# A recurrence kernel on one core: mixing, feeding and projecting in 64x64 tiles of the array, row halves added by VectorE, both projections ahead of the turn

## What is computed

```python
ms = mean(tokens ** 2, -1); x = tokens * rsqrt(ms + 1e-4) * norm_w     # 16 heads of 16
a_t = tanh(a)                                                          # (16 heads, 64, 64)
def step(state, x_t):                                                  # state: (batch, 16, 64)
    state = tanh(einsum('bhs,hst->bht', state, a_t) + einsum('bhd,hds->bhs', x_t, b))
    mixed = einsum('bhs,hsd->bhd', state, c) + skip * x_t
    return state, mixed
out = tokens + outs @ w_out.T + b_out                                  # then x = layernorm(x + out)
```

## Time and profile before

| | |
|---|---|
| runs | 2425.71 us median, 2422.68 to 2427.81 |
| profiled execution | 2422.44 us, its span 2420.7 us |
| mean granted clock | 0.980 |
| TensorE busy | 2310.3 us (95%) |
| VectorE busy | 1646.1 us (68%) |
| ScalarE busy | 1073.9 us (44%) |
| GpSimd busy | 1156.5 us (48%) |
| recurrence, first to last tanh | 1650.5 to 2204.9 us |

### The profile page before, as it was taken

How to read it: one execution, slowest core, us unless ns; L and a number is a source line. 1 busy time by engine, 2 the same in 40 slices (tenths; PEclk the granted TensorE clock), 3 DMA queues, 4 the chain that set the end, 5 groups by cost and what they waited for, 6 DMA issues and landing times. The chain is left out here.

```text
span 2420.7 us, 87690 instructions
## 1 busy us (share of the span) xinstructions
PE 2310.3 (95%) x35328; PEld 1553.8 (64%) x35328; DVE 1646.1 (68%) x4605; ACT 1073.9 (44%) x2707; POOL 1156.5 (48%) x1610
## 2 busy tenths in 40 slices
PE   6999999999999999869999999998999999997997
PEld 3565555556556665436666666666777777775775
DVE  3688888888877777548888888872444444443897
ACT  2656556665566666522222222222444444442444
POOL 2444454444444444337777777762333443331333
PEclk8999999999999999989999999997999999998999
DMA  2111111111111111020000000000100001101232
GB/s 86 56 36 44 45 45 45 45 45 41 45 45 45 45 45 36 28 69 27 31 30 30 30 30 26 31 22 22 35 30 30 30 30 34 31 28 46 79 87 78
DMA packets 91382, 100.88 MB, mean 42 GB/s; under 512 B 8625, under 2 KB 78033, under 8 KB 91217
## 3 DMA queue, kind: packets, MB, share of 16 engines
q1 hardware_dynamic: 91216, 98.67, 12.4%
HBM read 48.31 MB, written 33.55 MB: 34 GB/s over the span
## 5 line engine op out<-in xcount | busy, mean ns | idle before, releaser
L1427 ACT ACTIVATE r_state<-ps_state 128x64 f32<-128x64 f32 x1024 | 228.7, 223 | 335.6 <-PE ps_state L1524 330.0
L1521 PE MATMUL ps_state<-r_state,later_pairs_a 64*64 64x32 f32 x8192 | 340.9, 221 | 18.5 <-ACT r_state L1427 12.7
L1521 PEld LDWEIGHTS ps_state<-r_state,later_pairs_a 64*64 64x64 f32 x8192 | 287.6, 135 | 99.8 <-issue 81.4
L1524 PE MATMUL ps_state<-r_state,later_pairs_a 64*64 64x32 f32 x8192 | 340.9, 222 | 0.0
L399 DVE CUSTOM_DVE_ANT_0 ps_near<-ps_near,mask 128x512 f32<-128x512 f32 (+1 forms) x512 | 270.5, 590 | 92.3 <-PE ps_near L495 92.3
L273 POOL TENSOR_SCALAR_AFFINE_SELECT probsT<-probsT 128x512 f32<-128x512 f32 x256 | 159.4, 635 | 315.3 <-ACT probsT L382 173.6
L1524 PEld LDWEIGHTS ps_state<-r_state,later_pairs_a 64*64 64x64 f32 x8192 | 284.8, 135 | 0.0
L399 DVE CUSTOM_DVE_ANT_0 ps_far<-ps_far,mask 128x384 f32<-128x384 f32 (+1 forms) x512 | 198.8, 461 | 47.4 <-PE ps_far L495 46.4
L1234 PE MATMUL ps_down<-kept_w_downT,f_hT 128*128 128x256 f32 (+1 forms) x768 | 190.5, 390 | 1.9 <-ACT f_hT L1146 1.9
L1141 ACT ACTIVATE f_silu<-ps_gate 128x704 f32<-128x704 f32 x64 | 48.5, 757 | 313.8 <-PE ps_gate L1226 310.3
L503 PE MATMUL ps_far<-Q,K 32*128 32x256 f32 (+2 forms) x1536 | 175.8, 414 | 0.7 <-ACT probsT L379 0.5
(11 more groups left out here) (209 smaller groups left out, 5368.1 us busy)
## 6 DMA issues: line engine op xcount, KB each, us to landing
k_swap<-k_sin SPq DMA_DIRECT2D x128, 128.0 KB, 2.0
xT<-in_xT_dram SPq DMA_DIRECT2D x16, 512.0 KB, 3.6
xtok<-in_x_dram SPq DMA_DIRECT2D x16, 512.0 KB, 3.8
x_rows<-x SPq DMA_DIRECT2D x16, 512.0 KB, 2.8
f_x<-x_rows SPq DMA_DIRECT2D x64, 128.0 KB, 2.0
x_rows<-f_x SPq DMA_DIRECT2D x64, 128.0 KB, 1.7
r_x<-x_rows SPq DMA_DIRECT2D x64, 128.0 KB, 2.0
x_rows<-r_x SPq DMA_DIRECT2D x64, 128.0 KB, 1.9
```

The source lines that it names most:

```text
L1427: nc.scalar.activation(state[:, j % 2, banks, :, t, 0, :], sums[:, j % 2, banks, :, now], ACT.Tanh).then_inc(state_ready[t], 1)
L1521: nc.tensor.matmul(sums[half(v), j % 2, stays, c, now], A[half(v), 3 * q, c, :], last[half(v), stays, c, :], start=False, stop=True, skip_ ...
L1524: out = nc.tensor.matmul(sums[half(1 - v), j % 2, changes, c, now], A[half(v), 3 * q + 1 + was, c, :], last[half(v), changes, c, :], start ...
```

## The change

`pairs_b` and `pairs_c` get zeros, so that each product takes 64 rows of the array instead of 32 (feed) or 128 (mix), and 64 columns instead of 32 (mix). `project` becomes four matmuls, one for each quadrant. Where the contraction spans 128 rows (mix, project), upper and lower rows give separate sums in separate banks, and VectorE adds these with one more operation each. The banks of MIX and OUT change for that. PROJECTS and TURNS change places, VectorE adds z ahead of xT, and TensorE waits for its own last feed (inputs_in) in front of a tile's first step.

```diff
@@ LaterWeights
-        self.pairs_b = sb("pairs_b", [P, 2 * CC, STATE])
-        self.pairs_c = sb("pairs_c", [P, 6, CC, 2 * HEAD_DIM])
+        self.pairs_b = sb("pairs_b", [P, 2, 2 * CC, STATE])
+        self.pairs_c = sb("pairs_c", [P, 6, CC, 4 * HEAD_DIM])
@@ recurrence
-    TURN, MIX, OUT = 0, (1, 3), 2
+    TURN, MIX, OUT = 0, ((1, 3), (0, 2)), (1, 3)
@@ VectorE
-                            nc.vector.scalar_tensor_tensor(outs[:, s, c, :], xT[:, s, c, :], skip[:, c:c + 1], room[:, s, MIX[c], 0:P],
-                                                           ALU.mult, ALU.add).then_inc(outs_ready, 1)
+                            nc.vector.scalar_tensor_tensor(outs[:, s, c, :], xT[:, s, c, :], skip[:, c:c + 1], room[:, s, MIX[c][0], 0:P],
+                                                           ALU.mult, ALU.add).then_inc(outs_half, 1)
+                            dve.wait_ge(outs_half, 2 * i + (c - 1))
+                            nc.vector.tensor_tensor(outs[:, s, c, :], outs[:, s, c, :], room[:, s, MIX[c][1], 0:P], ALU.add).then_inc(outs_ready, 1)
+                        dve.wait_ge(out_full, i + 1)
+                        dve.wait_ge(twice_ready, i)
...
+                        nc.vector.tensor_tensor(z[:, s, :], room[:, s, OUT[0], :], x_twice[:, s, :], ALU.add).then_inc(z_half, 1)
+                        dve.wait_ge(z_half, i)
+                        nc.vector.tensor_tensor(z[:, s, :], room[:, s, OUT[1], :], z[:, s, :], ALU.add).then_inc(z_added, 1)
                     if exists(i, 1):
...
                     if exists(i, -1):
-                        dve.wait_ge(out_full, i + 1)
-                        dve.wait_ge(twice_ready, i)
...
-                        nc.vector.tensor_tensor(z[:, s, :], room[:, s, OUT, :], x_twice[:, s, :], ALU.add).then_inc(z_added, 1)
@@ TensorE, feed
-                        for v in range(2):
-                            for bank in range(BANKS):
-                                rows = slice(32 * bank, 32 * bank + 32)
-                                xT_now = xT[rows, s, c, :]
...
+                        for odd in range(2):
+                            for v in range(2):
+                                for r in range(2):
+                                    bank, weights_of = 2 * r + odd, B[half(r), odd, 2 * c + v, :]
+                                    xT_now = xT[half(r), s, c, :]
...
@@ project
-                    out = nc.tensor.matmul(room[:, s, OUT, :], outs[:, s, c, :], w_outT[:, c, :], start=(c == 0), stop=(c == CC - 1))
+                    for cols in range(2):
+                        for r in range(2):
+                            out = nc.tensor.matmul(room[half(cols), s, OUT[r], :], outs[half(r), s, c, half(cols)], w_outT[half(r), c, :],
+                                                   start=(c == 0), stop=(c == CC - 1), skip_group_check=True)
@@ mix
+                    for n in range(3):
+                        for cols in range(2):
+                            for r in range(2):
+                                into = room[half(cols), s, MIX[c][r], 0:P]
+                                weights_of = C[half(r), 3 * cols + n, c, :]
+                                if n == 0:
+                                    nc.tensor.matmul(into, weights_of, state[half(r), s, 2 * cols, c, :, 0, :], start=True, stop=False, skip_group_check=True)
+                                else:
+                                    out = nc.tensor.matmul(steps_of(into, n - 1), weights_of, state[half(r), s, 2 * cols + 1, c, n - 1::2, 0, :],
+                                                           start=False, stop=True, skip_group_check=True)
...
-                MIXES, PROJECTS, TURNS, FEEDS = (1, 3), (5, 9), 7, (13, 15)
+                MIXES, PROJECTS, TURNS, FEEDS = (1, 3), (5, 7), 9, (13, 15)
...
+                                if t == 0 and q == 0:
+                                    await_count(inputs_in, this_tile)
                                 recur(j, t, q, states)
```

More of the change, by code:

```diff
@@ L1459, in step @@
                                 dve.wait_ge(out_full, i - 1)
-                            nc.vector.scalar_tensor_tensor(outs[:, s, c, :], xT[:, s, c, :], skip[:, c:c + 1], room[:, s, MIX[c], 0:P],
-                                                           ALU.mult, ALU.add).then_inc(outs_ready, 1)
+                            nc.vector.scalar_tensor_tensor(outs[:, s, c, :], xT[:, s, c, :], skip[:, c:c + 1], room[:, s, MIX[c][0], 0:P],
[4 more added lines that the diff above has]
+                        dve.wait_ge(twice_ready, i)
+                        if later(i, -1, 2):
+                            dve.wait_ge(x3_ready, i - 2)
+                        nc.vector.tensor_tensor(z[:, s, :], room[:, s, OUT[0], :], x_twice[:, s, :], ALU.add).then_inc(z_half, 1)
+                        dve.wait_ge(z_half, i)
+                        nc.vector.tensor_tensor(z[:, s, :], room[:, s, OUT[1], :], z[:, s, :], ALU.add).then_inc(z_added, 1)
                     if exists(i, 1):
@@ L1533, in feed @@
                     for parity in range(2):
-                        for v in range(2):
-                            for bank in range(BANKS):
-                                rows = slice(32 * bank, 32 * bank + 32)
-                                xT_now = xT[rows, s, c, :]
[L1538 to L1543, removed]
+                        for odd in range(2):
[3 more added lines that the diff above has]
+                                    xT_now = xT[half(r), s, c, :]
+                                    if odd:
+                                        out = nc.tensor.matmul(steps_of(sums[half(v ^ parity), s, bank, c, :], parity), weights_of, steps_of(xT_now, parity),
+                                                               start=(c == 0 and parity == 0), stop=False, skip_group_check=True)
+                                    elif parity == 0:
+                                        nc.tensor.matmul(sums[half(v), s, bank, c, :], weights_of, xT_now,
+                                                         start=(c == 0), stop=False, skip_group_check=True)
                     return out
@@ L1601, in step @@
                                 if before:
-                                    fill(j, OUT, 9, c == 0)
+                                    fill(j, OUT[0], 9, c == 0)
                                 if c == 0:
@@ L1624, in recurrence_arrays @@
     pairs_a = np.zeros((P, 6, CC, STATE), np.float32)
-    pairs_b = np.zeros((P, 2 * CC, STATE), np.float32)
-    pairs_c = np.zeros((P, 6, CC, 2 * HEAD_DIM), np.float32)
+    pairs_b = np.zeros((P, 2, 2 * CC, STATE), np.float32)
+    pairs_c = np.zeros((P, 6, CC, 4 * HEAD_DIM), np.float32)
     for h in range(HEADS):
@@ L1629, in recurrence_arrays @@
         at = (h * HEAD_DIM) % P
-        pairs_b[at:at + HEAD_DIM, 2 * chunk + v, :] = b[h]
         side, changes = bank // 2, bank % 2
+        pairs_b[at:at + HEAD_DIM, changes, 2 * chunk + v, :] = b[h]
         for order in range(1 + changes):
@@ L1635, in recurrence_arrays @@
             pairs_a[rows, 3 * side + changes + order, chunk, :] = a[h]
-            pairs_c[rows, 3 * side + changes + order, chunk, v * HEAD_DIM:(v + 1) * HEAD_DIM] = c[h]
+            column = (2 * changes + v) * HEAD_DIM
+            pairs_c[rows, 3 * side + changes + order, chunk, column:column + HEAD_DIM] = c[h]
     columns = np.concatenate([f("norm_w").reshape(CC, P).T, f("skip").reshape(CC, P).T], 1)
```

8 lines of the change are left out of this document (3 added, 5 removed).

## The result

The changed kernel takes 2407.49 us (median of 4 runs, 2406.14 to 2415.08); the kernel before took 2426.22 in the same job (4 runs, 2422.68 to 2427.81). The ratio is 0.9941 [0.9921, 0.9961], a gain of 18.7 us where 25 were forecast. The time lies in the range, 7.0 us above the predicted one.

A forecast was written before the change was run, and what follows sets the result against it. TensorE's own time was taken to bound every round with an extra, down to a 0.88 us floor. Per tile -0.74 + 0.26 + 0.09 = -0.39 us, by 64 tiles -25 us: 2400.5 us, range 2383 to 2420 (8 in 10).

The forecast's parts named there:

- The projection: Project in four quadrants: 0.43 us against 0.72 net, two save 0.58 a tile; its round becomes 0.90, not 1.23.
- rival 4: The hole comes from any change of weights and banks, not of tile shape; +0.9 a tile, 2459 us; chance 0.03.
- Mix: Mix in 64x64 quadrants: 0.45 us against 0.45 net, nothing gained.
- Feed: Feed over 64 rows, half of them zeros: 0.45 us per quadrant against 0.49; two feeds save 0.08 a tile.
- The slow first pass: Step products behind mix, project and feed start at 0.06 instead of 0.08 us: 4 rounds save 0.08 a tile.
- The waits that the hole covered: Waits in the first feed and first mix rounds show more without a drain: +0.09 us a tile, between 0 and 0.15.
- the term for the new wait for inputs_in: TensorE's wait before each tile's first step: +0.37 us, or +0.15 at the loop's branch; average +0.26 a tile.
- Rival 3: The self-wait and the uncovered waits at their upper bounds: -0.14 us a tile, -9 us, 2417 us; chance 0.10.
- Rival 1: Weight loads in the open: each extra pass costs 0.028 us more, +0.39 a tile net, 2451 us; chance 0.09.
- the Trainium skill's rule: A weight load overlaps matmuls in flight only where the row group differs, so new extras would pay each load openly.
- Rival 2: VectorE's outs sum isn't ready for the projection: +0.4 us a tile eats the gain, 2426 us; chance 0.05.
- Rival 5: The clock: another rhythm shifts the early slow stretch some us, or costs hundreds if full clock isn't held (chance 0.02).

## Why the prediction was right, and where it was off

- **The projection held.** Forecast rounds of 0.90 instead of 1.23; measured 0.898 instead of 1.227. The hole of 0.15 in the earlier trace rows is gone: the last step pass starts at 1806.45, the projection at 1806.46, with other weights and banks, which is what rival 4 held to be the cause. Putting the full-array projection back gives the hole back, and rounds of 1.24 and 1.23.
- **Mix held.** Forecast nothing gained: 0.959 became 0.918 in the second round, 1.004 became 1.025 in the first, and with the old mix the tile is the same to 0.004.
- **Feed held as far as it can be seen alone.** The seventh round lost 0.039 by the table, which holds to about 0.015; forecast 0.04.
- **The slow first pass went, as forecast.** Behind a mix a quadrant's second step pass comes 0.03 after its first (L1531: 1805.14 and 1805.17), where it was 0.08. The first pass of an extra is slow instead: of the feed's 128-column passes the second starts 0.139 after the first (1811.101, 1811.240), the next pass 0.109 later. The two nearly cancel.
- **The waits that the hole covered do show.** The first round is 0.107 longer than the second now, 0.045 before, and it is 0.10 shorter without two of its waits (with the old feed). The shapes gave as much more than forecast: the projection's rounds 0.66 for 0.58 + 0.04, the second mix 0.04 for 0.02. So rounds 1 to 7 gave 0.704, where 0.70 less 0.09 for these waits was forecast.
- **The step that failed is the term for the new wait for inputs_in: 0.26 a tile forecast, 0.45 to 0.51 measured** (0.449 added to the kernel before; here 0.470 net of a feed that saves about 0.04). Two things were wrong in it.
  - The gap was too small. I had 0.52 from the last feed pass to the tile's first product: 0.22 for the pass, 0.15 for the hand-over, 0.15 for a second wait. The last feed pass starts at 1811.57 and the product at 1812.23, 0.66. In the events of TensorE's queue the wait for inputs_in is passed 0.30 after the pass starts, the state's wait 0.25 later, and the first weight load starts 0.07 after that. So the end of the pass and the wait behind it came out cheaper than forecast (0.30, not 0.37), but the second wait took 0.25 instead of 0.15, and the 0.10 from it to the first product weren't in the sum. The 0.25 are 0.15 up to the register instruction of L1514 and 0.10 from there to the wait. On average the gap was 0.15, and 0.41 behind the branch; now it is 0.66 in both tiles. That is +0.51 and +0.25, where I had +0.37 and +0.15: 0.12 too little a tile.
  - The hole behind the feed was taken off twice. The feed's 0.45 against 0.49 already puts the next pass 0.06 behind the last feed pass, and the +0.37 then takes off the whole 0.15 again. That is 0.09 more a tile. Some 0.04 remain; how much the second feed itself saves cannot be seen apart from the wait.
- **How much was luck.** The eighth round came out 0.25 longer than forecast and the other seven 0.09 shorter, so two misses partly cancel. The recurrence gained 15 us, not 25; that the medians gained 18.7 is 3.7 us that the account does not explain.
- **Rival 3**, waits at their upper bounds, had the right cause, though the 0.47 in the eighth round is over its bound of 0.45, and a poorer sum of the rest (its 9 us against 15 in the recurrence).
- **Rival 1 fell.** The projection's and mix's rounds leave no room for 0.028 a pass. The loads of the new feed run beside its 128-column matmuls. Weight loads of the changed kernel (PEld), which start while the 128-column matmuls (L1550, 1811.10 to 1811.56) run:

```profile
1811.07 0.24 PEld L1550 LDWEIGHTS ps_state<-r_xT,later_pairs_b 64*64 64x64 f32 x8
...
1811.24 0.18 PEld L1547 LDWEIGHTS ps_state<-r_xT,later_pairs_b 64*64 64x64 f32 x4
```

  So the Trainium skill's rule from "TensorE: Matmul & The Clock Gate", section "The mechanism", which the prediction weighed, does not describe this case: the loads at 1811.24 start while all four quadrants, and so the same row groups, have a 128-column matmul in flight, and the next pass still comes 0.109 after the last, the 0.11 worked out for the columns alone.
- **Rival 2 fell.** The second addition took 0.286, not 0.35, and outs was ready at 1806.04 and 1806.96, ahead of the projections at 1806.46 and 1807.36 (the second stands 0.90, a round, behind the first). No wait of TensorE names VectorE.
- **Rival 5** did not decide: the recurrence ran at the full clock from 1700 to 1800 us as in the earlier trace rows.

The new feed without the wait was not run. The reason for the wait, that the last feed and the next tile's first products add to the same sums and nothing else orders them in a uniform shape, is argued and not shown.

## What to carry to other kernels

Price a wait that an engine makes for its own last instruction by what it costs to start again from empty: its end, the wait itself, every satisfied wait behind it, and the first load; here 0.45 us a tile, more than half of what all the new shapes brought. When such a gap takes the place of an old one, take the old one off once. A change of tile shape costs a hole of 0.15 us here. But where a uniform shape needs a wait in its place, the old shape can be the cheaper one: the old feed without the wait is 27 us quicker than the new feed with it. Of a change with several parts, run each alone: here the projection brought 42 us, and the rest cost 23 of them.

## What the runs showed of the hardware

- A TensorE wait on a satisfied semaphore costs 0.15 us where the queue has no lead (eighth round 1.602 to 1.752). Where it has one, nothing shows: the projection, behind a wait for outs, starts 0.01 after the last step pass (1806.45, 1806.46).
- Behind the loop's branch TensorE's waits stand in the open: 0.40 us from the last pass to the next product with the old feed and no wait, 0.65 and 0.67 with one satisfied wait more.
- fp32 passes of 64x64 quadrants follow each other at 0.058 us with 16, 32 and 64 columns, at 0.109 with 128. With 128 columns the weight load is hidden; whether the load is what sets the 0.058 isn't shown.
- From the last pass of one tile shape to the first of another it is 0.15 us, in the same shape 0.01 to 0.06; with one shape for all products of a round the 0.15 is gone.
- The half-clock stretch at the FFN's start differs between traces of almost the same stage: 23.9 to 47.8 us between 1000 and 1620 (27.3 before, 47.8 after), with the recurrence's first tanh at 1647.9 to 1656.9. These 9 us are half of what was measured here, so only stretches behind it, or ratios over several runs, tell such changes apart.
